# Attention in a macaron block: the score tiles on the diagonal share PSUM banks, and a group's exponentials are cut into 48 strips in place of 56

## The chip, the cores and the metric

The kernel runs on one core of one Trainium2 chip. Its time is the device time of one execution in microseconds: the median of three runs before the change is 1180.17 us (1180.03 to 1180.23). The four compute engines (TensorE or PE, VectorE or DVE, ScalarE or ACT, GpSimd or POOL) and the queue engine (SyncE or SP) each run their own instructions in order and wait for one another on semaphores. Everything here is float32, except the queries and keys of the attention, which are float16 features.

## The reference

A macaron block: half a feed-forward layer with routing to 2 of 16 experts, causal attention, half a feed-forward layer again. The change is in the attention alone, for 2 batches of 2048 tokens and 16 heads.

```python
L_q, L_k = exterior(q1, q2), exterior(k1, k2)      # 6 numbers a head and token, normalized
attn = jnp.einsum('bqhc,bkhc->bhqk', L_q, L_k @ _J6.T) * 6.0 ** (-0.5)
attn = jnp.where(causal, attn, -jnp.inf)           # a query sees the keys up to itself
attn = jax.nn.softmax(attn, axis=-1)
v = (x @ W_v + b_v).reshape(B, T, H, 16)
out = jnp.einsum('bhqk,bkhd->bqhd', attn, v).reshape(B, T, D)
x = x + out @ W_o + b_o                            # x was normalized ahead of this
```

## The kernel before, in words

Four heads make a group; there are 4 groups a batch, so `ALL` = 8 groups one after the other, numbered 0 to 7. In a group the 2048 queries are cut into `QC` = 4 chunks of 512 columns, and the keys into 16 tiles of 128. A **unit** is one chunk against one key tile for all four heads, four score tiles of 128 keys by up to 512 queries. Chunk `qc` has `4 * qc + 4` units, 40 in a group; the last four key tiles of a chunk lie on the diagonal, and of them only 512, 384, 256 and 128 columns are computed.

The score tiles go through the engines as follows.

- PE computes them (`scores`, L1880): a product over 32 rows and 128 keys, with head h on rows 32h to 32h + 31. Two slots of three PSUM banks hold them. What fills one slot is a **strip**, at most three score tiles, and a step of a group is the work for one strip.
- ACT takes the exponential of one strip with one instruction (L2021), into a ring of 8 strips in SBUF (`probs`, the tensor `wide`). It must wait until PE has used what stood there.
- POOL zeroes the triangle above the diagonal in the masked units (L2037).
- PE multiplies the values with the exponentials (`weigh`, L1905; the trace shows two records for each of the four products of a unit, one a head), and adds a chunk up in bank 6 or 7. The values carry a part whose product is the sum of the exponentials.
- DVE divides (L2069 to L2080): copy, shuffle, reciprocal, product. PE projects with `W_o` (`project`, L1919), and DVE adds to the residual (L2094).

The order on PE is written out: in step i, `scores(i)`, then the `weigh` of the units whose `pv_step` is i, then what else is due (a projection, transposes of the routing). `scores(i)` waits for exponential i - 2. Before, `strips_of` chooses the strips by a dynamic program with a cost of 152 columns a strip. It keeps the order of the units and gives a strip the columns of its widest tile. `PV_LAGS` is a table of how many steps after its last strip each unit is weighed. The projections stand at the steps of `PROJECT_7`, `PROJECT_6` and `PROJECT_6_LATE`; the ones of `PROJECT_7` in every group but the first, the others in every second group.

Of the kernel before, what the change touches and what calls it, by code (L numbers as in the profile page):

```python
# [25 lines left out]
BT = 4  # L26
# [11 lines left out]
STRIP_RING, STRIP_WIDE = 8, 3  # L38
# [1219 lines left out]
def lines(nc, core, w, tag, ctx, y_slots, q_dram, k_dram, v_dram, lent):  # L1258
# [278 lines left out]
    def vector(dve):  # L1537
# [89 lines left out]
        def split_lines(n, ring):  # L1627
# [28 lines left out]
STRIP_COST = 152  # L1656


PV_LAGS = (5, 5, 4, 4,
# [3 lines left out]

PROJECT_7, PROJECT_6, PROJECT_6_LATE = (30, 34), (39, 45, 49, 54), (49, 51, 53, 54)


def strips_of(first_columns, wide, multiple):

    count = len(first_columns)
    best = [{0: (0, None)}]  # L1670
    for end in range(1, count + 1):
        here = {}
        for n in range(1, min(wide, end) + 1):
            cost = n * (QW - min(first_columns[end - n:end])) + STRIP_COST
# [12 lines left out]

def attend(nc, core, w, tag, ctx, lines_sem, rest, v_stored, q_dram, k_dram, v_dram, xn_rows, second, routing, second_w):
# [17 lines left out]
    score = [banks[:, WIDE * n:WIDE * (n + 1), :] for n in range(SLOTS)]  # L1706
    out_bank = [banks[:, 6 + qc % 2, :] for qc in range(QC)]
# [5 lines left out]
    per_chunk = QW // P  # L1713
    units = [(qc, kt, max(0, kt - per_chunk * qc) * P) for qc in range(QC) for kt in range(per_chunk * (qc + 1))]
    U = len(units)
    last_of = [max(u for u, v in enumerate(units) if v[0] == qc) for qc in range(QC)]
    diagonal = [u for u, (qc, kt, _) in enumerate(units) if kt >= per_chunk * qc]

    strips = strips_of([c0 for _, _, c0 in units for _ in range(HG)], WIDE, RING)
    N = len(strips)  # L1720
    strip_of = [i for i, (_, n, _) in enumerate(strips) for _ in range(n)]
    place_of = [i % RING * WIDE + j for i, (_, n, _) in enumerate(strips) for j in range(n)]
    last_strip = [strip_of[HG * u + HG - 1] for u in range(U)]
    first_strip = [strip_of[HG * (last_of[qc - 1] + 1 if qc else 0)] for qc in range(QC)]

    pv_step = [last_strip[u] + lag for u, lag in enumerate(PV_LAGS)]
    assert all(a <= b for a, b in zip(pv_step, pv_step[1:]))
    pv_at = {i: [u for u in range(U) if pv_step[u] == i] for i in range(max(pv_step) + 1)}
    for i in range(N):
        assert pv_step[(strips[i][0] + strips[i][1] - 1) // HG] <= i + RING - 2  # L1730
    pieces = []
    for u in diagonal:
        runs = []
        for h in range(HG):
            at = place_of[HG * u + h]
            if runs and runs[-1][1] == at:
                runs[-1][1] = at + 1
            else:
                runs.append([at, at + 1])
        pieces.append(runs)  # L1740
    masks_of = {u: sum(len(runs) for runs in pieces[:n + 1]) for n, u in enumerate(diagonal)}
    MASKS = masks_of[diagonal[-1]]
# [6 lines left out]
    def projected_before(two, qc, half):  # L1749
# [7 lines left out]
    weights_at, logits_at, logits_turn_at, count_at, exp_at = (GATE, 41), (GATE + 1, 41), (GATE + 1, 45), (GATE + 2, 52), (GATE + 2, 6)  # L1757
    assert max(i for g, i in (logits_at, logits_turn_at)) < min(PROJECT_6_LATE) and turn_at.keys().isdisjoint({(GATE + 1, i) for i in range(29, 38)})
    rest_uses = sorted([*turn_at, weights_at, logits_at, logits_turn_at, count_at])

    late_at = {(0, 4): 0, (0, 6): 1, (0, 12): 2, (0, 15): 3}
    late_bank = lambda part: banks[:, 7 - part // 2, :]
    kept_at = {(0, 5): 0, (0, 7): 1, (0, 13): 2, (0, 16): 3}
    copied_at = (0, 2)
    assert pv_step[last_of[0]] < 12 and pv_step[last_of[0] + 1] > 6 and pv_step[last_of[1] + 1] > 15
# [56 lines left out]
    def sync(sp):  # L1822
# [27 lines left out]
        for g in range(ALL - 1):  # L1850
            for m in range(QC - 1):
                sp.wait_ge(sem.scores_ready, N * g + last_strip[last_of[m]] + 1)
                sp.sem_inc(sem.load_turn, 1)
                load_q(sp, g + 1, m)
            for m in range(QC):
                sp.wait_ge(sem.pv_done, U * g + last_of[QC - 2] + 1 + (m + 1) * BT)
                sp.sem_inc(sem.load_turn, 1)
                load_kv(sp, g + 1, m)
                if g == GATE and m < QC - 1:
                    store_normal(m)  # L1860
            load_q(sp, g + 1, QC - 1)
            if g == GATE:
                store_normal(QC - 1)
            if g == GATE + 1:
                load_shared(sp)

    def tensor(pe):
        def scores(g, i):
            first, n, c0 = strips[i]
# [12 lines left out]
            last.then_inc(sem.scores_ready, 1)  # L1882

        def weigh(g, side, two, u, uses):
# [122 lines left out]
    def scalar(act):  # L2007
        def group(g, side, two):
            for i, (first, n, c0) in enumerate(strips):
                act.wait_ge(sem.scores_ready, N * g + i + 1)  # L2010
                if i >= RING:
                    held = (strips[i - RING][0] + strips[i - RING][1] - 1) // HG
                    act.wait_ge(sem.pv_done, U * g + held + 1)
                elif later(g):
                    held = (strips[N + i - RING][0] + strips[N + i - RING][1] - 1) // HG
                    act.wait_ge(sem.pv_done, U * (g - 1) + held + 1)
# [3 lines left out]
                at = i % RING * WIDE  # L2020
# [6 lines left out]
        groups(group)  # L2027

    def gpsimd(pool):
        def group(g, side, two):  # L2030
            for u, runs in zip(diagonal, pieces):
                c0 = units[u][2]
                pool.wait_ge(sem.exp_done, N * g + last_strip[u] + 1)
                pool.sem_inc(sem.mask_turn, 1)
                for begin, end in runs:
                    part = probs[:, begin:end, c0:c0 + P]
                    pool.affine_select(out=part, in_=part, compare_op=ALU.is_ge, fill=0.0, base=0,  # L2037
                                       pattern=[[0, end - begin], [1, P]], channel_multiplier=-1).then_inc(sem.masked, 1)
# [682 lines left out]
```

## Time and profile before the change

| | us |
|---|---|
| median of three runs | 1180.17 |
| the profiled execution | 1177.99 |
| its span in the trace | 1176.3 |
| attention, first to last exponential (L2021) | 378.8 to 903.3 |
| busy: PE, ACT, DVE, POOL | 1036.9, 884.8, 774.8, 435.5 |
| exponentials of the attention (448) | 505.5 |

Of the span, 378.8 us lie ahead of the first exponential and 273 us behind the last. The first feed-forward layer and the second one are not touched. In the attention nothing is read or written in bulk: the 16 DMA engines are busy for 5 to 17% of a group.

### The profile page before, as it was taken

The numbers are of one execution on the slowest core, as the hardware profiler recorded it, in microseconds if no ns is written. First come the engines' busy times: TensorE is split into PE (matmuls) and PEld (weight loads), VectorE is DVE, ScalarE is ACT, GpSimd is POOL, SyncE is SP. The second block draws the span as 40 slices with busy tenths as digits, with TensorE's granted clock in tenths as the row PEclk, the third lists the DMA queues.
The fourth block names the chain that finished last, engine by engine and source line by source line (L and its number), as shares of the span: only waits on it lengthen the run. The fifth ranks groups of instructions, "written<-read, shape, count | busy, mean of one in ns | idle before, by whom it ended". The sixth has DMA issues, their size and how long they took to land.

```text
span 1176.3 us, 23514 instructions
## 1 busy us (share of the span) xinstructions
PE 1036.9 (88%) x7487; PEld 557.7 (47%) x7487; DVE 774.8 (66%) x1565; ACT 884.8 (75%) x1314; POOL 435.5 (37%) x531
## 2 busy tenths in 40 slices
PE   4998999898886888998889898988889998999996
PEld 3457999755553211222122122222123568898854
DVE  6897777768996314443244557476579778777866
ACT  4336777646888999999999999989998336677720
POOL 1004666377720323321111122430121435577755
PEclk9999999989998899999999999999999999999998
DMA  8902555446766101010201022020200854566655
GB/s 289 289 27 60 166 172 167 144 121 197 214 193 215 52 20 53 19 50 10 64 10 46 23 69 76 22 80 8 58 1 1 272 185 149 158 185 186 178 170 152
DMA packets 125716, 133.78 MB, mean 114 GB/s; under 512 B 13224, under 2 KB 111888, under 8 KB 125616
## 3 DMA queue, kind: packets, MB, share of 16 engines
q1 hardware_dynamic: 109056, 90.95, 24.5%
q0 software_dynamic: 14448, 39.47, 12.2%
q10 hardware_dynamic: 2112, 2.10, 0.5%
q8 instruction: 55, 0.90, 0.3%
q14 instruction: 45, 0.37, 0.1%
HBM read 80.43 MB, written 52.04 MB: 113 GB/s over the span
## 4 chain that ended last, share of the span: by engine, by line
PE 25%; ACT 23%; issue 19%; DVE 9%; POOL 2%; DVEq 1%; DMA 1%; ACTq 0%; POOLq 0%
ACT wide L2021 21%; PE banks L2388 6%; PE banks L2313 4%; PE banks L1905 3%; PE banks L2400 3%; PE banks L1880 2%; POOL f_region L1341 2%; PE banks L2322 2%; PE banks L1919 1%; PE banks L2376 1%; DVE x_res L1595 1%; DVE wide L1622 1%; DVEq L2596 1%; PE banks L1433 1%; DVE attn_lines_parts L202 1%
## 5 line engine op out<-in xcount | busy, mean ns | idle before, releaser
L2021 ACT ACTIVATE wide<-banks 128x1536 f32<-128x1536 f32 (+1 forms) x448 | 505.5, 1282 | 14.6 <-PE banks L1880 14.4
L1905 PE MATMUL banks<-wide,attn_attend_v_now 128*32 128x512 f32 (+3 forms) x2560 | 298.6, 542 | 0.1
L2037 POOL TENSOR_SCALAR_AFFINE_SELECT wide<-wide 128x512 f32<-128x512 f32 (+2 forms) x176 | 89.5, 523 | 444.3 <-ACT wide L2021 443.9
L1880 PE MATMUL banks<-attn_attend_q_now,attn_attend_k_now 32*128 32x512 f16 (+3 forms) x1280 | 158.8, 357 | 68.1 <-ACT wide L2021 64.3
L1880 PEld LDWEIGHTS banks<-attn_attend_q_now,attn_attend_k_now 32*128 32x128 f16 x1280 | 43.2, 91 | 321.2 <-ACT wide L2021 297.6
L651 POOL DMA_INDIRECT f_region<-xn_rows,f_token_of x79 | 79.1, 1001 | 126.0 <-DVE f_token_of L882 83.7
L2388 PE MATMUL banks<-f_xnt 128*128 128x128 f32 x752 | 101.7, 278 | 9.8 <-DVE f_more L2614 7.2
L2074 DVE RECIPROCAL below<-below 128x512 f32<-128x512 f32 x32 | 107.3, 3353 | 1.1
L2388 PEld LDWEIGHTS banks<-f_xnt 128*128 128x128 f32 x752 | 91.3, 191 | 15.3 <-ACT f_xnt L2466 8.8
L2069 DVE COPY sums<-banks 128x512 f32<-128x512 f32 x32 | 22.1, 691 | 109.9 <-PE banks L1905 109.1
L2496 POOL DMA_INDIRECT last_rows_in<-xn_rows,f_spare x72 | 69.7, 968 | 64.3 <-DVE f_stage L2557 23.7
L2094 DVE TENSOR_TENSOR x_res<-banks,x_res 128x512 f32<-128x512 f32 x30 | 20.7, 690 | 105.9 <-PE banks L1919 105.9
L2466 ACT ACTIVATE f_xnt<-last_w_all 128x514 f32 x94 | 59.4, 632 | 37.7 <-issue 27.4
L520 PE MATMUL banks<-f_region,wide 128*128 128x128 f32 x632 | 85.4, 279 | 0.0
L1905 PEld LDWEIGHTS banks<-wide,attn_attend_v_now 128*32 128x32 f32 x2560 | 51.6, 108 | 68.6 <-issue 61.7
L520 PEld LDWEIGHTS banks<-f_region,wide 128*128 128x128 f32 x632 | 77.8, 194 | 1.8 <-issue 0.6
L1341 POOL DMA_INDIRECT f_region<-y_slots,attn_lines_rows_of x64 | 69.8, 1090 | 23.6 <-issue 17.1
L619 ACT ACTIVATE wide<-f_w_all 128x514 f32 x79 | 50.0, 632 | 30.5 <-issue 29.5
L2599 DVE COPY last_w_down<-last_w_all 128x512 f32 x94 | 42.3, 450 | 23.2 <-issue 17.1
L2400 PE MATMUL banks<-last_w_down,f_more 128*128 128x256 f32 x188 | 56.3, 381 | 1.4 <-DVE f_more L2614 1.4
L897 DVE COPY wide<-f_w_all 128x512 f32 x79 | 38.1, 482 | 20.6 <-issue 20.2
L531 PE MATMUL banks<-wide 128*128 128x256 f32 x158 | 47.1, 381 | 0.4 <-DVE wide L910 0.4
(365 smaller groups left out, 1774.1 us busy)
## 6 DMA issues: line engine op xcount, KB each, us to landing
y_half<-f_xnt SPq DMA_DIRECT2D x94, 128.0 KB
y_slots<-wide SPq DMA_DIRECT2D x79, 128.0 KB, 1.7
attn_v<-f_more SPq DMA_DIRECT2D x32, 256.0 KB, 3.7
attn_attend_v_now<-attn_v SPq DMA_DIRECT2D x32, 256.0 KB, 3.1
x_res<-L_attn_x SPq DMA_DIRECT2D x8, 512.0 KB, 7.6
xn_rows<-f_w_all SPq DMA_DIRECT2D x8, 512.0 KB, 4.5
attn_q<-attn_lines_q_out SPq DMA_DIRECT2D x8, 512.0 KB, 3.4
attn_k<-attn_lines_k_out SPq DMA_DIRECT2D x8, 512.0 KB, 4.0
```

The source lines that it names most:

```text
L520: last = pe.matmul(bank[2 + m][:, f * P:(f + 1) * P], w_up[:, at, col_at:col_at + INTER], rows_t[:, m, c * P:(c + 1) * P], start=(c == 0), ...
L651: pool.indirect_dma_start(out=rows_in[:, n % ROUND, :], out_offset=None, in_=xn_rows, in_offset=bass.IndirectOffsetOnAxis(ap=token_of[:, n ...
L1341: pool.indirect_dma_start(out=back[:, q, j, k, :], out_offset=None, in_=y_slots, in_offset=bass.IndirectOffsetOnAxis(ap=rows_of[:, q, j, k ...
L1880: last = pe.matmul(score[i % SLOTS][:, j, c0:QW], k_now[rows, kt * P:(kt + 1) * P], q_now[rows, qc * QW + c0:(qc + 1) * QW], start=True, s ...
L1905: last = pe.matmul(out_bank[qc][rows, c0:QW], v_now[:, kt, rows], probs[:, place_of[HG * u + h], c0:QW], start=(kt == 0), stop=(u == last_ ...
L2021: act.activation(probs[:, at:at + n, c0:QW], score[i % SLOTS][:, 0:n, c0:QW], ACT.Exp, scale=SCALE).then_inc(sem.exp_done, 1)
L2037: pool.affine_select(out=part, in_=part, compare_op=ALU.is_ge, fill=0.0, base=0, pattern=[[0, end - begin], [1, P]], channel_multiplier=-1 ...
L2074: dve.reciprocal(below[:], below[:]).then_inc(sem.chain_step, 1)
L2388: last = pe.matmul(bank[2 + m][:, f * P:(f + 1) * P], w_up[:, at, col_at:col_at + INTER], rows_t[:, m, c * P:(c + 1) * P], start=(c == 0), ...
L2400: pe.matmul(bank[4 + m][:, 0:D], prod_t[:, at, :], w_down[:, at, 0:D], start=True, stop=True).then_inc(sem.y_done, 1)
L2466: act.activation(w_up[:, n % ROUND, :], w_all[:, bass.ds(expert, 1), 0:UP].rearrange("p o f -> p (o f)"), ACT.Copy).then_inc(sem.up_kept, 1)
L2496: pool.indirect_dma_start(out=rows_in(n), out_offset=None, in_=xn_rows, in_offset=bass.IndirectOffsetOnAxis(ap=s.token_of[:, place_of_turn ...
```

## The change

The strips are made by `units_and_banks`. Every chunk's masked units stand behind the first 0, 3, 5 or 9 of its other key tiles, and ahead of the rest of them. The 16 masked score tiles of a chunk take 12 banks and 4 strips: in the first two strips each bank but the third holds a tile of 512 columns, in the last two a tile of 384 columns and, in the remaining 128 columns, the tile of the last unit of the same head. The third bank of each of the four holds a tile of 256 columns. So a strip is 1536 or 1280 columns, all of them contiguous, and ACT reads it as one row (before: a pattern of up to three parts). The table `PV_LAGS` goes; a unit is weighed 2 steps after its last strip, or 4 where it is masked, and never ahead of the one before. POOL makes 10 small cuts a chunk. The projections, and the routing's transposes that are woven in, are given new steps.

```diff
-STRIP_COST = 152
-PV_LAGS = (5, 5, 4, 4,
...
-PROJECT_7, PROJECT_6, PROJECT_6_LATE = (30, 34), (39, 45, 49, 54), (49, 51, 53, 54)
-def strips_of(first_columns, wide, multiple):
...
+LAG, MASKED_LAG = 2, 4
+UNITS_AHEAD = (0, 3, 5, 9)
+HALF_HEADS = (2, 0, 3, 1)
+PROJECT_7, PROJECT_6, PROJECT_6_LATE = (24, 28), (33, 38, 42, 46), (42, 43, 45, 46)
+def units_and_banks():
+    units, banks = [], []
+    for qc in range(QC):
+        own = range(BT * qc, BT * qc + BT)
+        ahead, behind = range(UNITS_AHEAD[qc]), range(UNITS_AHEAD[qc], BT * qc)
+        for kt in (*ahead, *own, *behind):
+            units.append((qc, kt, max(0, kt - BT * qc) * P))
+        of = {kt: len(units) - 1 - n for n, kt in enumerate(reversed((*ahead, *own, *behind)))}
+        banks += [[(of[kt], h, 0)] for kt in ahead for h in range(HG)]
+        assert len(banks) % STRIP_WIDE == 0
+        one, two, three, four = (of[kt] for kt in own)
+        for n, half in enumerate(HALF_HEADS):
+            for h in (2 * n % HG, 2 * n % HG + 1):
+                banks.append([(one, h, 0)] if n < 2 else [(two, h, 0), (four, h, QW - P)])
+            banks.append([(three, half, 0)])
+        banks += [[(of[kt], h, 0)] for kt in behind for h in range(HG)]
+    return units, banks
...
-    pv_step = [last_strip[u] + lag for u, lag in enumerate(PV_LAGS)]
+    pv_step = [last_strip[u] + (MASKED_LAG if u in diagonal else LAG) for u in range(U)]
+    pv_step = [max(pv_step[:u + 1]) for u in range(U)]
...
-    turn_at = {(GATE, 45): (0, 0), (GATE, 49): (0, 1), (GATE, 52): (1, 0), (GATE, 54): (1, 1),
-               (GATE + 1, 13): (2, 0), (GATE + 1, 16): (2, 1), (GATE + 1, 24): (3, 0), (GATE + 1, 28): (3, 1)}
+    turn_at = {(GATE, 38): (0, 0), (GATE, 42): (0, 1), (GATE, 44): (1, 0), (GATE, 46): (1, 1),
+               (GATE + 1, 10): (2, 0), (GATE + 1, 12): (2, 1), (GATE + 1, 19): (3, 0), (GATE + 1, 23): (3, 1)}
...
         def scores(g, i):
...
-            for j in range(n):
-                qc, kt, _ = units[(first + j) // HG]
-                h = (first + j) % HG
-                rows = slice(h * HR, (h + 1) * HR)
-                last = pe.matmul(score[i % SLOTS][:, j, c0:QW], k_now[rows, kt * P:(kt + 1) * P],
-                                 q_now[rows, qc * QW + c0:(qc + 1) * QW], start=True, stop=True)
+            for j, parts in enumerate(score_banks[WIDE * i:WIDE * (i + 1)]):
+                for u, h, column in parts:
+                    qc, kt, c0 = units[u]
+                    rows = slice(h * HR, (h + 1) * HR)
+                    last = pe.matmul(score[i % SLOTS][:, j, column:column + columns(u)], k_now[rows, kt * P:(kt + 1) * P],
+                                     q_now[rows, qc * QW + c0:(qc + 1) * QW], start=True, stop=True)
...
-                act.activation(probs[:, at:at + n, c0:QW], score[i % SLOTS][:, 0:n, c0:QW], ACT.Exp, scale=SCALE).then_inc(sem.exp_done, 1)
+                act.activation(probs_flat[:, at:at + width_of[i]], score_flat[i % SLOTS][:, 0:width_of[i]], ACT.Exp, scale=SCALE
+                               ).then_inc(sem.exp_done, 1)
...
+                for n in range(BT):
+                    at = (strip + n) % RING * WIDE
+                    pool.wait_ge(sem.exp_done, N * g + strip + n + 1)
+                    pool.sem_inc(sem.mask_turn, 1)
+                    cut(pool, probs[:, at:at + 2, 0:P])
+                    if n >= 2:
+                        cut(pool, probs[:, at:at + 2, QW - P:QW])
+                    cut(pool, probs[:, at + 2:at + 3, 0:P])
```

On PE, the order around the end of chunk 1 in group 0, before. `attn_attend_q_now,attn_attend_k_now` are scores (their last number is the columns), `wide,attn_attend_v_now` a unit that is weighed, `ident,f_xnt` transposes left over from the layer ahead.

```order
L1880 MATMUL banks<-attn_attend_q_now,attn_attend_k_now 128x128 x3
L1880 MATMUL banks<-attn_attend_q_now,attn_attend_k_now 128x512 x3
L1905 MATMUL banks<-wide,attn_attend_v_now 32x384 x4
L1880 MATMUL banks<-attn_attend_q_now,attn_attend_k_now 128x512 x3
L1905 MATMUL banks<-wide,attn_attend_v_now 32x256 x4
L1880 MATMUL banks<-attn_attend_q_now,attn_attend_k_now 128x512 x3
L1905 MATMUL banks<-wide,attn_attend_v_now 32x128 x4
L1880 MATMUL banks<-attn_attend_q_now,attn_attend_k_now 128x512 x3
L1905 MATMUL banks<-wide,attn_attend_v_now 32x512 x4
```

The same place now, steps 12 to 16, with the score products of two strips in the first row.

```order
L1872 MATMUL banks<-attn_attend_q_now,attn_attend_k_now 128x512 x6
L1898 MATMUL banks<-wide,attn_attend_v_now 32x512 x4
L1872 MATMUL banks<-attn_attend_q_now,attn_attend_k_now 128x512 x6
L1898 MATMUL banks<-wide,attn_attend_v_now 32x384 x4
L1898 MATMUL banks<-wide,attn_attend_v_now 32x256 x4
L1898 MATMUL banks<-wide,attn_attend_v_now 32x128 x4
L1898 MATMUL banks<-wide,attn_attend_v_now 32x512 x4
L1872 MATMUL banks<-attn_attend_q_now,attn_attend_k_now 128x512 x3
L1898 MATMUL banks<-wide,attn_attend_v_now 32x512 x4
```

The three narrow masked units stood one a step, each behind the scores of a strip; now all three and the next unit of 512 columns stand in one step, with no scores between them. This is so at steps 7, 15, 27 and 47 of every group.

On ACT, one group's exponentials before, from chunk 2 on (`128x3x384` is a strip of three parts of 384 columns).

```order
L2021 ACTIVATE wide<-banks 128x1536 x12
L2021 ACTIVATE wide<-banks 128x3x384
L2021 ACTIVATE wide<-banks 128x2x384
L2021 ACTIVATE wide<-banks 128x3x256
L2021 ACTIVATE wide<-banks 128x3x128
L2021 ACTIVATE wide<-banks 128x128
L2021 ACTIVATE wide<-banks 128x1536 x17
L2021 ACTIVATE wide<-banks 128x1024
```

The same group now, from chunk 1's last strip on.

```order
L2012 ACTIVATE wide<-banks 128x1536 x7
L2012 ACTIVATE wide<-banks 128x1280 x4
L2012 ACTIVATE wide<-banks 128x1536 x16
L2012 ACTIVATE wide<-banks 128x1280 x4
L2012 ACTIVATE wide<-banks 128x1536 x4
```

A group had 37 strips of 1536 columns and 19 of 1152 down to 128, and 70,528 columns; it has 32 of 1536 and 16 of 1280, and 69,632 columns.

## Rows read from the trace of the kernel before

**Rows 1.** The page's costliest groups, attention's.
```profile
L2021 ACT ACTIVATE wide<-banks 128x1536 f32<-128x1536 f32 (+1 forms) x448 | 505.5, 1282 | 14.6 <-PE banks L1880 14.4
L1905 PE MATMUL banks<-wide,attn_attend_v_now 128*32 128x512 f32 (+3 forms) x2560 | 298.6, 542 | 0.1
L1880 PE MATMUL banks<-attn_attend_q_now,attn_attend_k_now 32*128 32x512 f16 (+3 forms) x1280 | 158.8, 357 | 68.1 <-ACT wide L2021 64.3
```

**Rows 2.** Stretches of one group: length, busy PE PEld DVE ACT POOL, clock, DMA, GB/s.
```profile
448.83:513.39 64.56, 58.44 (x508) 15.81 (x504) 28.48 (x29) 63.10 (x57) 20.58 (x27) 1.00 0.12 35
513.39:577.42 64.03, 54.41 (x492) 13.23 (x488) 24.64 (x24) 62.98 (x58) 10.77 (x22) 1.00 0.11 32
...
706.01:774.66 68.65, 62.73 (x544) 18.21 (x540) 38.90 (x49) 63.53 (x57) 21.16 (x28) 1.00 0.17 52
774.66:839.16 64.50, 54.85 (x494) 13.30 (x490) 41.27 (x68) 63.28 (x59) 11.44 (x22) 1.00 0.14 41
839.16:903.80 64.64, 58.55 (x509) 15.93 (x505) 49.71 (x82) 63.15 (x56) 12.54 (x24) 1.00 0.05 14
...
378.79:448.78 69.99, 54.74 (x482) 13.77 (x486) 19.91 (x24) 67.97 (x63) 19.66 (x24) 0.93 0.14 45
```

**Rows 3.** Exponentials alone, stretches from one start to another: busy (x), clock, DMA.
```profile
550.67:573.28 22.61, 22.61 (x17) 1.00 0.14 42
514.67:515.57 0.90, 0.90 (x2) 1.00 0.01 2
515.57:516.58 1.01, 1.01 (x2) 1.00 0.00 0
516.58:517.27 0.69, 0.69 (x2) 1.00 0.00 0
```

**Rows 4.** Timeline of PE, group 2, steps 35 to 39: start, us, engine, what.
```profile
551.62 0.39 PE L1880 MATMUL banks<-attn_attend_q_now,attn_attend_k_now 32*128 32x512 f16 x3
551.94 0.85 PE L1905 MATMUL banks<-wide,attn_attend_v_now 128*32 128x384 f32 x8
552.72 0.39 PE L1880 MATMUL banks<-attn_attend_q_now,attn_attend_k_now 32*128 32x512 f16 x3
553.04 0.86 PE L1905 MATMUL banks<-wide,attn_attend_v_now 128*32 128x256 f32 x16
553.84 0.39 PE L1880 MATMUL banks<-attn_attend_q_now,attn_attend_k_now 32*128 32x512 f16 x3
554.16 1.07 PE L1905 MATMUL banks<-wide,attn_attend_v_now 128*32 128x512 f32 x8
555.15 0.39 PE L1880 MATMUL banks<-attn_attend_q_now,attn_attend_k_now 32*128 32x512 f16 x3
```

**Rows 5.** Timeline, group 2, full strips: three exponentials from 541.60, scores of step 27.
```profile
541.60 4.24 ACT L2021 ACTIVATE wide<-banks 128x1536 f32<-128x1536 f32 x3
...
543.21 0.39 PE L1880 MATMUL banks<-attn_attend_q_now,attn_attend_k_now 32*128 32x512 f16 x3
```

**Rows 6.** Timeline, group 2 to 3: an exponential that waited for its scores.
```profile
576.93 0.39 PE L1880 MATMUL banks<-attn_attend_q_now,attn_attend_k_now 32*128 32x512 f16 x3 [0.35 <-ACT wide L2021]
...
577.37 1.45 ACT L2021 ACTIVATE wide<-banks 128x1536 f32<-128x1536 f32 x1 [0.20 <-PE banks L1880]
```

**Rows 7.** Timeline of PE, group 2: a projection, and the scores behind it.
```profile
547.50 1.13 PE L1919 MATMUL banks<-attend_w_o,heads 128*128 128x256 f32 x4
548.56 0.28 PE L1880 MATMUL banks<-attn_attend_q_now,attn_attend_k_now 32*128 32x256 f16 x3
```

**Rows 8.** Timeline: the first scores, five tiles of heads 0, 1, 2, 3, 0.
```profile
375.76 0.14 PEld L1880 LDWEIGHTS banks<-attn_attend_q_now,attn_attend_k_now 32*128 32x128 f16 x5 [2.37 <-issue]
375.79 1.01 PE L1880 MATMUL banks<-attn_attend_q_now,attn_attend_k_now 32*128 32x512 f16 x5 [2.13 <-ACT attn_lines_k_out L1496]
```

**Rows 9.** The same view around those first scores.
```profile
376.00:380.00 4.00, 0.80 (x5) 0.00 (x0) 3.34 (x5) 2.95 (x4) 0.00 (x0) 0.50 1.04 337
...
384.00:388.00 4.00, 3.98 (x28) 1.52 (x27) 0.00 (x0) 3.57 (x5) 1.40 (x3) 0.50 0.00 0
```

**Rows 10.** Groups by shape on POOL, the masks.
```profile
L2037 POOL TENSOR_SCALAR_AFFINE_SELECT wide<-wide 128x512 f32<-128x512 f32 x80 | 52.7, 660 | 431.4 <-ACT wide L2021 431.4
L2037 POOL TENSOR_SCALAR_AFFINE_SELECT wide<-wide 128x128 f32<-128x128 f32 x48 | 14.0, 293 | 12.9 <-ACT wide L2021 12.4 <-issue 0.3
```

**Rows 11.** The page's DMA issues: KB each, median us to landing.
```profile
attn_attend_v_now<-attn_v SPq DMA_DIRECT2D x32, 256.0 KB, 3.1
```

**Rows 12.** The chain that ended last, behind the attention: start, us, what.
```profile
906.27 0.70 DVE sums L2069
907.15 0.73 DVE below L2072
907.91 3.36 DVE below L2074
911.30 0.76 DVE sums L2077
912.08 0.69 DVE heads L2080
```

**Rows 13.** Timeline of the attention's end.
```profile
903.17 2.36 PE L1905 MATMUL banks<-wide,attn_attend_v_now 128*32 128x512 f32 x32
...
903.29 0.49 ACT L2021 ACTIVATE wide<-banks 128x384 f32<-128x384 f32 x1 [0.61 <-PE banks L1880]
...
906.27 0.69 DVE L2069 COPY sums<-banks 128x512 f32<-128x512 f32 x1
```

More of the change, by code:

```diff
@@ L1710, in attend @@
     q_loaded, kv_loaded = ring_semaphores(nc, f"{tag}_q_loaded", QC), ring_semaphores(nc, f"{tag}_kv_loaded", QC)
-    per_chunk = QW // P
-    units = [(qc, kt, max(0, kt - per_chunk * qc) * P) for qc in range(QC) for kt in range(per_chunk * (qc + 1))]
-    U = len(units)
+    units, score_banks = units_and_banks()
+    U, N = len(units), len(score_banks) // WIDE
+    assert len(score_banks) == N * WIDE and N % RING == 0
     last_of = [max(u for u, v in enumerate(units) if v[0] == qc) for qc in range(QC)]
-    diagonal = [u for u, (qc, kt, _) in enumerate(units) if kt >= per_chunk * qc]
@@ L1719, in attend @@
[L1719 to L1724, printed above, removed]
-    pv_step = [last_strip[u] + lag for u, lag in enumerate(PV_LAGS)]
-    assert all(a <= b for a, b in zip(pv_step, pv_step[1:]))
+    diagonal = [u for u, (qc, kt, _) in enumerate(units) if kt >= BT * qc]
@@ new lines, in attend @@
+    first_column = lambda u: units[u][2]
+    columns = lambda u: QW - first_column(u)
+    place_of = {(u, h): (b % (RING * WIDE), column) for b, parts in enumerate(score_banks) for u, h, column in parts}
+    strip_of = {(u, h): b // WIDE for b, parts in enumerate(score_banks) for u, h, _ in parts}
+    last_strip = [max(strip_of[u, h] for h in range(HG)) for u in range(U)]
+    first_strip = [min(strip_of[u, h] for u, v in enumerate(units) if v[0] == qc for h in range(HG)) for qc in range(QC)]
@@ L1728, in attend @@
+    width_of = [(WIDE - 1) * QW + max(column + columns(u) for u, _, column in score_banks[WIDE * i + WIDE - 1]) for i in range(N)]
+    held_by = [max(u for parts in score_banks[WIDE * i:WIDE * (i + 1)] for u, _, _ in parts) for i in range(N)]
+    pv_step = [last_strip[u] + (MASKED_LAG if u in diagonal else LAG) for u in range(U)]
+    pv_step = [max(pv_step[:u + 1]) for u in range(U)]
     pv_at = {i: [u for u in range(U) if pv_step[u] == i] for i in range(max(pv_step) + 1)}
     for i in range(N):
-        assert pv_step[(strips[i][0] + strips[i][1] - 1) // HG] <= i + RING - 2
@@ L1731, in attend @@
[L1731 to L1742, printed above, removed]
+        assert pv_step[held_by[i]] <= i + RING - 1
+    blocks = [(qc, strip_of[last_of[qc - 1] + 1 + UNITS_AHEAD[qc] if qc else 0, 0]) for qc in range(QC)]
@@ L1744, in attend @@
+    MASKS_OF_BLOCK = 10
+    masks_of = {u: MASKS_OF_BLOCK * units[u][0] + (3 if units[u][2] == 0 else MASKS_OF_BLOCK) for u in diagonal}
+    MASKS = MASKS_OF_BLOCK * QC
     two_of_0, four_of_1 = ((0, 0), (0, 1)), ((1, 0), (1, 1), (2, 0), (2, 1))
@@ L1904, in weigh @@
                 rows = slice(h * HR, (h + 1) * HR)
-                last = pe.matmul(out_bank[qc][rows, c0:QW], v_now[:, kt, rows], probs[:, place_of[HG * u + h], c0:QW],
+                place, column = place_of[u, h]
+                last = pe.matmul(out_bank[qc][rows, c0:QW], v_now[:, kt, rows], probs[:, place, column:column + columns(u)],
                                  start=(kt == 0), stop=(u == last_of[qc]))
@@ L2008, in group @@
         def group(g, side, two):
-            for i, (first, n, c0) in enumerate(strips):
+            for i in range(N):
                 act.wait_ge(sem.scores_ready, N * g + i + 1)
                 if i >= RING:
-                    held = (strips[i - RING][0] + strips[i - RING][1] - 1) // HG
-                    act.wait_ge(sem.pv_done, U * g + held + 1)
+                    act.wait_ge(sem.pv_done, U * g + held_by[i - RING] + 1)
                 elif later(g):
-                    held = (strips[N + i - RING][0] + strips[N + i - RING][1] - 1) // HG
-                    act.wait_ge(sem.pv_done, U * (g - 1) + held + 1)
+                    act.wait_ge(sem.pv_done, U * (g - 1) + held_by[N + i - RING] + 1)
                 if (g, i) == exp_at:
@@ L2027, in scalar, with cut @@
         groups(group)
+    def cut(pool, part):
+        pool.affine_select(out=part, in_=part, compare_op=ALU.is_ge, fill=0.0, base=0,
+                           pattern=[[0, part.shape[1]], [1, P]], channel_multiplier=-1).then_inc(sem.masked, 1)
     def gpsimd(pool):
         def group(g, side, two):
[L2031 to L2038, printed above, removed]
+            for qc, strip in blocks:
+                u = last_of[qc]
+                for n in range(BT):
[6 more added lines that the diff above has]
+                    cut(pool, probs[:, at + 2:at + 3, 0:P])
                 if g < 2 and u in (last_of[1], last_of[2]):
```

35 lines of the change are left out of this document (9 added, 26 removed), and 3 rows, old and new, of the table PV_LAGS.

## The prediction

> **What bounds the kernel now.** I read the page's list of costly groups first, then the attention stretch by stretch, then the timeline of one group. The list [rows 1] shows the attention's three large terms: 505.5 us of exponentials on ACT, 298.6 us of products with the values and 158.8 us of scores on PE. PE waits 64.3 us for ACT there, ACT only 14.4 us for PE. So ACT leads, and PE follows with little to spare. By stretch [rows 2] a group takes 64.03 us (even) or 64.56 us (odd), PE is busy for 54 to 58 us of it and ACT for 63, at the full clock (1.00). Group 5, into which the routing's products are woven, takes 68.65, group 0, with a slow start, 69.99.
>
> Busy time hides what ACT waits, since its record runs a little into the next one. The starts say more [rows 3]: 17 strips of 1536 columns take 22.61 us, 1.33 each. 1024 columns take 0.90, 1152 take 1.01, 768 take 0.69. That is a line: 0.05 us a strip and 0.833 us per 1000 columns. A group's 37 full strips are then 49.2 us, and its 19 others (4 of 1152, 2 of 1024, 5 of 768, 3 of 512, 4 of 384, 1 of 128) 12.4, together 61.6. The measured 64.03 is 2.4 us more: that is what ACT waits in a group, at the narrow strips, where an exponential is shorter than PE's step.
>
> **PE's step** is what the change has to be weighed with. In [rows 4] scores take 0.32 us to the products behind them (551.62 to 551.94), a unit of 512 columns 0.99 to the next scores (554.16 to 555.15), of 384 columns 0.78, of 256 and 128 together 0.80. Each of these ends holds about 0.10 us that is paid once, when the engine goes back to scores (the start of the scores behind a unit against the spacing of its products). So a step with one full unit is 1.31 to 1.33 us, exactly as long as ACT's 1.33. PE has no speed in reserve in such a step, only a lead. The lead: scores of step 27 start at 543.21, exponential 25 at 541.60 and 26 one strip later, at 542.93 [rows 5]. So scores start 0.27 us after the exponential before last has started its successor; an exponential that waits starts 0.44 us behind its scores [rows 6]. A strip is ready 0.27 + 0.44 = 0.71 us after the start of the one before it, 0.62 us ahead of need.
>
> **The change part by part**, for one group.
>
> *Strips.* 32 of 1.33 and 16 of 1280 columns. The trace has no strip of 1280; the bounds are its neighbours, 1.01 (1152) and 1.33 (1536), and the line gives 1.12, which I take. Sum 42.5 + 17.9 = 60.4 us, 1.2 less than 61.6. The narrow strips' waits, 2.4 us, go too. If PE kept up, a group would take 60.4.
>
> *The heavy step.* Steps 7, 15, 27 and 47 now hold the products of 384, 256, 128 and 512 columns. From the scores to the next scores: 0.32 + (0.78 - 0.10) + (0.80 - 0.10) + 0.99 = 2.69 us. The step before each is empty, so PE comes in with its full lead. The next exponential starts at 2.69 + 0.44 = 3.13 after the scores of the heavy step; ACT could start it at 2 x 1.33 - 0.27 = 2.39. It waits 0.74 us, four times: 3.0 us.
>
> *The steps behind it.* After steps 7 and 47 come two steps with a full unit each, PE 1.33, while ACT has strips of 1280, 1.12. With no lead left, 4 x 0.21 = 0.8 us. After 15 and 27 the strips are full, and this costs nothing. Then an empty step restores the lead.
>
> *Scores of one head behind one another.* Strips 3 and 4 of each masked block hold five tiles, on rows of heads 0, 0, 1, 1, 3. The trace has such a pair once: five tiles of heads 0, 1, 2, 3, 0 [rows 8], where one 512-column record is 0.6 us and the five together 1.01. The second tile of head 0 came 0.4 us later, at a clock of 0.50 [rows 9], so a tile on the same rows waits for the columns of the first. At full clock, heads in order, the chain is 384 + 384 + 256 columns at 0.42 us per 1000, 0.43 us in place of 0.21, and 0.2 later. It counts where PE has no lead, once after step 7 and once after 47: 0.4 us. Bounds: 0, and 0.3 for all columns in a row.
>
> The Trainium skill, "TensorE: Matmul & The Clock Gate", Part 3, "The mechanism", says that a weight load overlaps products in flight only on other row groups. In [rows 8] all five loads lie within 0.14 us, the fifth beside the product of its own rows, so the trace doesn't agree. By the rule each pair would also pay a load of some 0.09 us, 0.18 a strip and about 3 us over the kernel. My sum goes without it.
>
> *Projections.* One costs 1.06 us [rows 7], 0.10 of it the return to scores. At step 24 nothing else stands and the lead covers it. Step 28 has a unit too and follows the heavy step and a full one, without lead: 0.32 + 0.89 + 1.06 = 2.27 against 1.33, 0.94 us of waiting. In odd groups step 33 is alike but with a lead: 2.27 - 1.33 - 0.60 = 0.3. Step 42 stands between strips of 1280, behind the scores of one head: 0.4.
>
> *Masks.* 10 cuts a chunk in place of 5 or 6. One block is 0.29 us and four are 0.66 [rows 10]; two blocks lie between, about 0.41. A strip's cuts sum to 1.1 us, the units are weighed three strips later, so this is hidden. If it weren't, PE would stand with every unit behind it. The last keys and values of a group to come free, tiles 8 to 11, do so at step 49 and are read from the next group's step 13 on, 12 strips or 15 us later; such a load lands in 3.1 us [rows 11]. DVE's chain of a chunk, 906.27 to 912.77 [rows 12], 6.5 us, has 6 strips (8 us) at the tightest place, chunk 3 to chunk 0.
>
> *Sum.* Even group: 60.4 + 3.0 + 0.8 + 0.4 + 0.9 = 65.5, plus 0.1 where a strip of 1280 uses up the lead: 65.6, 1.6 more than now. Odd: 66.3, 1.8 more. Groups 2 and 4: 3.2; group 6 (64.50 now): 1.1; groups 1 and 3: 3.6. Group 5 has its projections at other steps and 4.1 us of extra waits now; I see as many after, 0. Group 0 has no projections, and chunk 3's heavy step counts in the next group: 60.4 + 2.2 + 0.4 + 0.2 against 61.6 + 2.4, -0.8; its first heavy step falls near 388 us, up to which the clock is 0.50 [rows 9], and 1.3 us longer products there make it +0.5. Group 7 from first to last exponential: 66.3 less the last strip (1.33) and the wait behind it (0.74), 64.2 against 64.1 now, +0.1. The end: now the last exponential starts at 903.29, and DVE copies at 906.27, 3.0 us later, held up by its own work [rows 13]; this copy is on the last chain [rows 12]. Then, PE has the heavy step and two full units left: 0.27 + 0.32 + 0.68 + 0.70 + 3 x 0.90 + 0.1 = 4.8 after exponential 46, so 3.5 after exponential 47, with DVE free. +0.5. Sum: 3.2 + 1.1 + 3.6 + 0.5 + 0.1 + 0.5 = 9.0 us. The rounding of the small waits (each cost that I took low by a few hundredths recurs 32 times) leans upwards, so I take 10. The profiled execution took 1177.99 us, 1.7 above its span and 2.2 below the median of the runs; 1188 by its own time, 1190 by the median.
>
> **The rivals.**
>
> A. *ACT alone decides.* PE's lead spans the heavy step, and every group takes 60.4: 7 x 3.8 + 4 = 31 us less, 1149. For it: ACT waits only 14.4 us now, PE waits 64.3. Against it: those 64 us lie in empty steps, and two PSUM slots let PE run no more than 0.6 us ahead.
>
> B. *The changed order costs less than written*: the pair of one head overlaps (-0.4 a group), and projection and unit pack tighter (the 0.10 is paid less often). -0.7 x 8: 1184. The other end of the same uncertainty, half of the waits real, gives no change, 1180.
>
> C. *A second wait behind the heavy step*: in group 0 more than one of its steps falls into the slow clock; in groups 5 and 7 DVE's routing work delays copies for which the woven products and projections now wait after fewer steps; and the load of the skill's rule. +2, +2, +3: 1197.
>
> **How the numbers follow.** My forecast has 0.62, A 0.05, B 0.14 (of it 0.04 for about no change), C 0.17; 0.02 for a partial gain between A and B. A measurement tells 0.2%, 2.4 us, from no change. Slower by more than that is the forecast, C and most of B, 0.90; the same 0.04; faster 0.06. The range runs from B to a little over C, 1184 to 1198; it leaves out A and the small cases, and the top of C.
>
> **What would show it.** The exponentials' own time falls to about 60.4 a group by starts, 483 us in all, while a group grows to 65.6 or 66.3. ACT's waits for scores rise from 14.4 to some 35 to 45 us, in pieces of 0.7 at exponentials 8, 16, 28 and 0, and 0.9 at 29. The timeline shows 2.7 us between the scores of steps 7 and 8. Wrong would be: a 1280 strip far from 1.12; no wait at exponential 8; waits of PE on masks or on DVE; a group under 64.

## The result, and the profile after

The changed kernel takes 1212.03 us (median of four runs, 1202.82 to 1214.77) against 1180.1 before (median of four as well): 1.0261 times as long, interval 1.0203 to 1.0319. That is slower, as forecast, but three times the forecast 10 us and outside the range of 1184 to 1198. The profiled execution took 1214.2 us.

The page's costliest groups after, beside [rows 1]:

```profile
L2012 ACT ACTIVATE wide<-banks 128x1536 f32<-128x1536 f32 (+1 forms) x384 | 499.1, 1416 | 54.7 <-PE banks L1872 51.8
L1898 PE MATMUL banks<-wide,attn_attend_v_now 128*32 128x512 f32 (+3 forms) x2560 | 309.7, 589 | 0.0
L2022 POOL TENSOR_SCALAR_AFFINE_SELECT wide<-wide 128x256 f32<-128x256 f32 (+1 forms) x320 | 114.1, 386 | 438.0 <-ACT wide L2012 435.4
L1872 PE MATMUL banks<-attn_attend_q_now,attn_attend_k_now 32*128 32x512 f16 (+3 forms) x1280 | 158.2, 376 | 75.0 <-ACT wide L2012 65.1
```

ACT's own work fell from 505.5 to 499.1 us, but its waits for scores rose from 14.4 to 51.8. PE's products with the values, the same number of the same shapes, rose from 298.6 to 309.7. The second line is the one to stop at: work that didn't change takes longer.

One row a group (groups 0 to 7, the last up to its last exponential), with the columns of [rows 2]:

```profile
380.06:452.99 72.93, 57.70 (x497) 15.24 (x501) 20.20 (x24) 67.36 (x54) 23.11 (x44) 0.84 0.14 43
452.99:520.55 67.56, 59.37 (x508) 16.91 (x509) 28.39 (x29) 62.24 (x48) 23.18 (x44) 0.95 0.11 32
520.55:590.88 70.33, 59.54 (x492) 15.26 (x493) 24.25 (x23) 62.34 (x49) 13.69 (x40) 0.88 0.11 31
590.88:659.49 68.61, 60.35 (x508) 17.02 (x508) 32.61 (x41) 62.34 (x49) 13.89 (x40) 0.93 0.11 32
659.49:730.17 70.68, 61.59 (x510) 16.59 (x511) 34.97 (x56) 62.15 (x48) 16.86 (x41) 0.88 0.15 46
730.17:799.84 69.67, 62.02 (x544) 18.73 (x545) 36.67 (x48) 62.76 (x48) 23.89 (x45) 0.98 0.15 47
799.84:870.43 70.59, 59.80 (x494) 14.75 (x495) 39.56 (x63) 62.44 (x50) 14.00 (x40) 0.88 0.14 42
870.43:938.42 67.99, 57.71 (x473) 15.82 (x473) 48.93 (x82) 60.99 (x47) 18.78 (x42) 0.92 0.05 14
```

The granted clock was 1.00 in groups 1 to 7 before; it is 0.88 to 0.98 now. Groups 1 to 6 take 67.6 to 70.7 us where I had 65.6 and 66.3. From first to last exponential the attention takes 558.4 us in place of 524.5, 33.9 of the 36.2 us between the two profiled executions; 1.3 lie ahead of it and 0.8 behind.

PE in group 3, from the unit of step 1 to the scores of step 8 (start, us, what, and the idle time before it):

```profile
592.07 1.07 PE L1898 MATMUL banks<-wide,attn_attend_v_now 128*32 128x512 f32 x8
593.07 0.81 PE L1872 MATMUL banks<-attn_attend_q_now,attn_attend_k_now 32*128 32x384 f16 x10
594.90 0.39 PE L1872 MATMUL banks<-attn_attend_q_now,attn_attend_k_now 32*128 32x512 f16 x3 [1.02 <-ACT wide L2012]
595.94 0.39 PE L1872 MATMUL banks<-attn_attend_q_now,attn_attend_k_now 32*128 32x512 f16 x3 [0.65 <-POOL wide L2022]
596.26 1.06 PE L1898 MATMUL banks<-wide,attn_attend_v_now 128*32 128x512 f32 x8
597.28 0.49 PE L1872 MATMUL banks<-attn_attend_q_now,attn_attend_k_now 32*128 32x512 f16 x3
598.62 0.61 PE L1872 MATMUL banks<-attn_attend_q_now,attn_attend_k_now 32*128 32x512 f16 x3 [0.85 <-ACT wide L2012]
599.16 4.50 PE L1898 MATMUL banks<-wide,attn_attend_v_now 128*32 128x384 f32 x32
603.59 0.61 PE L1872 MATMUL banks<-attn_attend_q_now,attn_attend_k_now 32*128 32x512 f16 x3
```

and the same stretch by busy time and clock (steps 2 to 4 with the scores of step 5; step 5's unit to the scores of step 7; the heavy products; what follows), with the exponential that waited:

```profile
593.07:596.26 3.19, 1.50 (x21) 0.45 (x17) 2.87 (x4) 3.10 (x4) 1.88 (x6) 1.00 0.51 147
596.26:599.16 2.90, 2.05 (x17) 0.36 (x14) 2.67 (x2) 2.90 (x3) 0.79 (x3) 0.70 0.66 200
599.16:603.59 4.43, 4.43 (x35) 1.39 (x33) 1.40 (x3) 2.09 (x2) 0.00 (x0) 0.50 0.02 4
603.59:607.50 3.91, 3.69 (x36) 0.79 (x32) 3.84 (x3) 3.04 (x3) 1.14 (x4) 0.91 0.00 0
```
```profile
604.25 1.24 ACT L2012 ACTIVATE wide<-banks 128x1280 f32<-128x1280 f32 x1 [2.99 <-PE banks L1872]
```

Steps 2 to 4 hold scores and nothing else: PE is busy for 1.50 of 3.19 us. In the next stretch the clock falls to half (1.2 GHz), at about 597.4 by its mean of 0.70 over 596.26 to 599.16, and the heavy step is taken at half clock, 4.43 us of products in place of the 2.4 of my sum. ACT idles for 2.99 us ahead of exponential 8; by starts, the way I had counted, it is 3.16 us late, not 0.74. The trace's record of the clock has twenty such falls between the first and the last exponential, eighteen of them behind the idle steps 2 to 4, 10 to 12 and 22 to 24. The kernel before has none after its slow start.

### The profile page after: what moved, and what is told of

It reads as the page before. It is cut to its first block, busy times and chain, and to the rows that moved or that the text cites. A ratio compares the mean times of both kernels' runs of the same rounds, so it can differ in the third digit from the quotient of the medians.

```text
span 1212.2 us, 23530 instructions
## 1 busy us (share of the span) xinstructions
PE 1058.3 (87%) x7487; PEld 569.8 (47%) x7487; DVE 771.3 (64%) x1565; ACT 879.0 (73%) x1250; POOL 458.2 (38%) x675
## 3 DMA queue, kind: packets, MB, share of 16 engines
q1 hardware_dynamic: 109056, 90.95, 23.7%
## 4 chain that ended last, share of the span: by engine, by line
PE 38%; ACT 14%; issue 12%; DVE 12%; POOL 2%; DVEq 1%; DMA 1%; ACTq 0%; POOLq 0%
PE banks L1898 14%; ACT wide L2012 13%; PE banks L2386 6%; PE banks L1872 5%; PE banks L2311 4%; PE banks L2398 3%; PE banks L1912 2%; POOL f_region L1341 2%; PE banks L2320 2%; DVE x_res L1595 1%; PE banks L2374 1%; DVE wide L1622 1%; DVEq L2594 1%; DVE attn_lines_parts L202 1%; DVE attn_lines_line L1633 1%
## 5 line engine op out<-in xcount | busy, mean ns | idle before, releaser
L2012 ACT ACTIVATE wide<-banks 128x1536 f32<-128x1536 f32 (+1 forms) x384 | 499.1, 1416 | 54.7 <-PE banks L1872 51.8
L1898 PE MATMUL banks<-wide,attn_attend_v_now 128*32 128x512 f32 (+3 forms) x2560 | 309.7, 589 | 0.0
L2022 POOL TENSOR_SCALAR_AFFINE_SELECT wide<-wide 128x256 f32<-128x256 f32 (+1 forms) x320 | 114.1, 386 | 438.0 <-ACT wide L2012 435.4
L1872 PEld LDWEIGHTS banks<-attn_attend_q_now,attn_attend_k_now 32*128 32x128 f16 x1280 | 39.0, 92 | 316.6 <-ACT wide L2012 218.6
L1898 PEld LDWEIGHTS banks<-wide,attn_attend_v_now 128*32 128x32 f32 x2560 | 64.7, 118 | 86.0 <-issue 79.5
L2494 POOL DMA_INDIRECT last_rows_in<-xn_rows,f_spare x72 | 69.9, 971 | 65.5 <-DVE f_stage L2555 23.7
```

The lines of the kernel that those rows point to most:

```text
L1872: last = pe.matmul(score[i % SLOTS][:, j, column:column + columns(u)], k_now[rows, kt * P:(kt + 1) * P], q_now[rows, qc * QW + c0:(qc + 1) ...
L2012: act.activation(probs_flat[:, at:at + width_of[i]], score_flat[i % SLOTS][:, 0:width_of[i]], ACT.Exp, scale=SCALE).then_inc(sem.exp_done, 1)
L2494: pool.indirect_dma_start(out=rows_in(n), out_offset=None, in_=xn_rows, in_offset=bass.IndirectOffsetOnAxis(ap=s.token_of[:, place_of_turn ...
```

## The experiments

All of these ran on another chip, on which the layers outside the attention take some 70 to 87 us longer (653.8 us of the changed kernel's span on the first chip, 723.6 to 741.1 in the eight profiles here): the kernel before takes 1261.54 us in the first set (23 runs) and 1253.78 in the second (19). So ratios are read within a set, and beside them the **attention time**, first to last exponential in the profile; it was 524.5 us before and 558.4 after, both on the first chip; the kernel before has no profile on the second. "Waits" are differences of exponentials' starts less the strip's own time (0.05 us and 0.833 us per 1000 columns). My first theory was that idle steps make the clock fall (1); the rivals were that the heavy step costs this by itself (2), or that the new strips do (3).

### Idle steps filled

```diff
+        def fill(g, side, two, i):
+            if g in (0, 5) or i not in (2, 3, 4, 10, 11, 12):
+                return
...
+            for _ in range(3):
+                pe.matmul(banks[:, 6, :], k_now[:, 0:P], k_now[:, 0:QW], start=True, stop=True)
```

> The changed kernel with three extra products of 128 rows, 128 keys and 512 columns (float16, into the idle bank 6, result unused) behind the scores of steps 2, 3, 4, 10, 11 and 12 of groups 1, 2, 3, 4, 6 and 7. They add PE work and remove only idleness. Theory 1 (the clock falls because steps 2 to 4 and 10 to 12 leave PE idle, and the heavy steps 7 and 15 then run at half clock): the granted clock in those groups returns to 1.00 at steps 7 and 15, the waits there shrink from 2 to 3 us to 0.5 to 0.8, a group takes 65 to 66.5 us in place of 68 to 70.5, and the whole 1190 to 1200 us (groups 0 and 5 unchanged). Rival, theory 2 (the heavy step itself, whatever stands before it, costs 2 to 3 us, through the products' queue or the masks): time unchanged at 1203 to 1215 or longer by what the extra products take.

Measured: 1.0117 times before (1.0060 to 1.0174), attention 541.1 us. In all six groups where they were filled, the falls at steps 2 to 7 and 10 to 15 are gone, and the waits at exponentials 8 and 16 are 0.59 us each. Ten falls in place of twenty are left, all where nothing was filled: group 0, group 5, and around steps 23, 24 and 45. So more work on PE makes the kernel faster (554.3 us of attention unfilled on this chip, see below); theory 2 predicted no gain or a loss.

### The rest of the idle steps filled

```diff
+            six, seven = i in (2, 3, 4, 10, 11, 12), i in (22, 23)
+            late = i in (43, 44) and side == 0 and g != GATE
```

> The changed kernel with idle steps filled as in the first filled run, and also steps 22 and 23 of every group, 43 and 44 of groups 0, 2 and 6, and 2 to 4 of group 5; the extra products' result is unused. Theory 1 (idle steps make the clock fall): of the ten falls that the first filled run kept, those at steps 23, 24 and 44 and in group 5 go, leaving group 0's. Attention falls from 541.1 to about 528 to 533 us, which is what my step arithmetic gave at full clock (525 to 536), and every group but 0 and 5 has clock 1.00 and takes 65 to 66 us. Theory 2: the waits at 24, 25 and 47 stay.

Measured: 1.0093 (1.0059 to 1.0126), attention 534.4 us. Groups 1 to 3, and PE's heavy step in group 3:

```profile
476.20:541.50 65.30, 61.68 (x532) 17.91 (x528) 28.43 (x29) 62.12 (x49) 23.48 (x44) 1.00 0.11 33
541.50:606.40 64.90, 59.16 (x522) 15.54 (x519) 24.29 (x23) 61.99 (x48) 13.69 (x40) 1.00 0.12 34
606.40:671.80 65.40, 61.78 (x532) 17.99 (x536) 32.53 (x41) 62.17 (x49) 14.13 (x40) 1.00 0.11 33
```
```profile
609.72 0.39 PE L1872 MATMUL banks<-attn_attend_q_now,attn_attend_k_now 32*128 32x384 f16 x5
...
614.52 2.36 PE L1898 MATMUL banks<-wide,attn_attend_v_now 128*32 128x384 f32 x32
616.81 0.39 PE L1872 MATMUL banks<-attn_attend_q_now,attn_attend_k_now 32*128 32x512 f16 x3
```

The heavy products take 2.29 us to the next scores, against 4.43 in the changed kernel, and a group 65.0 or 65.3. These groups are what my prediction described: the same order with the clock at 1.00. The whole run is not quite that. I expected one fall to be left, in group 0; there are three, in groups 0, 5 and 7:

```profile
430.40:433.80 3.40, 3.40 (x31) 1.07 (x27) 0.54 (x1) 1.44 (x2) 0.87 (x1) 0.50 0.07 19
754.70:758.10 3.40, 3.40 (x22) 0.47 (x23) 0.35 (x1) 2.48 (x2) 0.00 (x0) 0.50 0.13 39
935.60:942.40 6.80, 6.42 (x39) 2.86 (x43) 3.12 (x13) 3.15 (x3) 2.13 (x3) 0.50 0.01 2
```

Beside the same places without a fall they cost 1.5 us at exponential 16 of group 0 (2.12 against 0.59 in the other groups), 1.0 at exponential 14 of group 5 (no wait there in the first filled run) and 1.2 at exponential 47 of group 7 (1.45 against 0.29). Attention is 9.9 us longer than the 524.5 of before (the medians of this set differ by 10.9). Less these 3.7 us, the order at full clock throughout would cost about 6.2, an estimate; my sum had 8.5 for the attention.

### The changed kernel again, in the same set

> The changed kernel, unchanged, beside the others on one chip. Attention 553 to 562 us, 20 or so falls of the clock; 25 to 35 us slower than before. If the falls were an accident of the first chip, the time would be within 10 to 15 us of before.

Measured: 1.0226 (1.0134 to 1.0317), 28 us by this ratio and 23.7 at the medians, attention 554.3 us, 17 falls. In one set, then, 19.9 us of attention lie between the order with its idle steps and the order with them filled (12.8 us between the medians of whole runs). The runs also show it by themselves: their mean granted clock goes with their time, 1202.82 us at 0.956, 1209.85 at 0.951, 1214.2 and 1214.77 at 0.945 on the first chip.

### One unit a step earlier

```diff
+    pv_step = [5, 6, 7, 7, 7, 8, 9, 13, 14, 15, 15, 15, 16, 17, 19, 20, 21, 25, 26, 27, 27,
+               27, 28, 29, 31, 32, 33, 35, 36, 37, 39, 40, 41, 45, 46, 47, 47, 47, 48, 49]
```

The changed kernel has 5, 7, 7, 7, 7 at the start of this list, and so at each of the chunks: one masked unit of each goes a step earlier.

> The changed kernel with one difference: the masked unit of 384 columns is weighed one step earlier (steps 6, 14, 26, 46), so the heavy step holds 0.68 us less, and the idle steps 2 to 4 and 10 to 12 stay as they are. Theory 1: the clock still falls about as often (mean granted clock of the groups 0.88 to 0.97, as now), and the time falls by the smaller heavy step only, some 15 to 20 us of the waits at 7, 15, 27 and 47 (2.4 us a group at full clock), to 1190 to 1199 us. Theory 2 (the heaviness alone makes the clock fall or the wait long): the clock returns to 1.00 and the time to under 1185 us.

Measured: 1.0067 (1.0035 to 1.0099), attention 530.8 us, 12 falls. Less heavy, 23.5 us shorter than the 554.3 of the changed kernel on this chip, and the clock still falls. It gained more than I expected, and it does not single out a theory: the step moved fills one gap besides.

### All masked units a step earlier

```diff
-LAG, MASKED_LAG = 2, 4
+LAG, MASKED_LAG = 2, 3
```

> The changed kernel with MASKED_LAG 3 in place of 4: masked units one step earlier. The step that held 2.5 units of products is split in 1.5 and 1, and one of the three idle steps (4, 12) now has a unit. Theory 1: fewer falls of the clock than in the changed kernel (two idle steps in a row in place of three), mean clock of the groups 0.97 to 1.00, heavy waits gone, group 62 to 64 us, whole kernel 1168 to 1182 us. Theory 2 (heaviness alone) gives the same side but cannot give a clock under 1.00; a clock that still falls with no heavy step is for theory 1.

Measured: 0.9969 (0.9940 to 0.9998), attention 514.8 us, 2 falls, groups mostly 62.4 to 63.7. One number in one line takes the kernel from 2% slower to no slower. With 0.3% it is at the edge of what can be told.

### The products spread

```diff
-    pv_step = [last_strip[u] + (MASKED_LAG if u in diagonal else LAG) for u in range(U)]
-    pv_step = [max(pv_step[:u + 1]) for u in range(U)]
+    pv_step = [5, 6, 7, 7, 8, 10, 11, 12, 14, 15, 16, 16, 17, 18, 20, 21, 23, 25, 26, 27,
+               27, 29, 30, 31, 32, 33, 35, 36, 37, 38, 39, 41, 42, 45, 46, 47, 48, 49, 50, 51]
```

> The changed kernel with its strips, masks and projections, but a table of steps for the products with the values: at most one full unit a step, none of the steps 2 to 4 and 10 to 12 in a row empty. Theory 1 and the arithmetic of steps: no heavy step and no idle stretch, clock 1.00, a group takes 60.5 to 62 us, and the whole kernel 1155 to 1163 us, faster than both. Theory 3 (the new strips themselves cost more than the line of 0.05 us and 0.833 us per 1000 columns, or tiles that share a bank slow PE or ACT): a group stays over 64 us and the kernel over 1180.

Measured: 0.9886 (0.9858 to 0.9914), 14 us faster than before, attention 509.2 us. The clock stays at 1.00 from group 1 to step 45 of group 7. So the strips are good, and theory 3 falls: with them unchanged, another table of steps takes 45 us off the attention. It is a little less than I expected, because the odd groups take 62.92 us and not under 62.

### Idleness by itself

```diff
+                if u in (5, 6, 7):
+                    last = pe.matmul(out_bank[qc][rows, QW - 32:QW], v_now[:, kt, rows], probs[:, place, QW - 32:QW], start=False, stop=False)
+                    continue
```

> The spread kernel with work left out: the products with the values of units 5, 6 and 7 (steps 10, 11 and 12 of each group) cover the last 32 columns only, so the output is not the reference's. No step is heavy. Theory 1: steps 10 to 12 are idle but for their scores, the clock falls there in most groups, and the full units of steps 14 to 17 at half clock cost ACT 1 to 3 us a group: attention as long as in the spread run or longer (509 to 525 us), although 24 products fewer are computed. Theory 2 (only a heavy step costs): the clock stays at 1.00, attention 509 us or less.

Measured: 0.9975 (0.9944 to 1.0006), attention 514.8 us, 5.6 us longer than the spread kernel of the first set with less to compute. The clock falls at this place in every one of the eight groups. Group 2, steps 1 to 8, steps 9 to 12 (step 9 has no unit in this table), the fall, and after:

```profile
537.50:547.50 10.00, 9.33 (x92) 2.17 (x92) 5.50 (x5) 10.00 (x10) 3.34 (x10) 1.00 0.36 105
547.50:552.10 4.60, 2.27 (x44) 0.90 (x40) 4.23 (x6) 4.60 (x6) 2.30 (x7) 1.00 0.01 5
552.10:558.90 6.80, 6.04 (x44) 1.44 (x44) 2.06 (x2) 6.69 (x5) 1.03 (x4) 0.50 0.08 22
558.90:564.00 5.10, 4.84 (x44) 0.86 (x36) 4.25 (x4) 4.36 (x5) 0.00 (x0) 1.00 0.00 0
```

PE was busy for 2.27 of 4.60 us, with no heavy step anywhere near, and 6.8 us at half clock followed. The fall needs only the idleness. What it costs depends on what comes then: here mostly single units, 0.4 to 1.6 us of waits at exponentials 15 to 17 of groups 1 to 4, 6 and 7, where the spread kernel has none; in the changed kernel the heaviest step of the chunk, up to 3.2 us each.

### The version that beats both

The spread table, and the odd groups' projections at steps without a full unit:

```diff
-PROJECT_7, PROJECT_6, PROJECT_6_LATE = (24, 28), (33, 38, 42, 46), (42, 43, 45, 46)
+PROJECT_7, PROJECT_6, PROJECT_6_LATE = (24, 28), (34, 40, 44, 47), (40, 43, 44, 47)
-               (GATE + 1, 10): (2, 0), (GATE + 1, 12): (2, 1), (GATE + 1, 19): (3, 0), (GATE + 1, 23): (3, 1)}
+               (GATE + 1, 10): (2, 0), (GATE + 1, 13): (2, 1), (GATE + 1, 19): (3, 0), (GATE + 1, 23): (3, 1)}
```

> The spread table of the earlier run, with the projections of the odd groups moved from steps 33, 38, 42, 46 to 34, 40, 44, 47 (group 5: 40, 43, 44, 47), steps with no product of values or a small one, and one transpose of group 5 from step 12 to 13. Arithmetic of steps: an odd group takes 62.92 us in the spread run against 60.92 for an even one, because a projection beside a full unit overruns ACT by 0.3 to 0.9; that goes. Attention 509.2 us there, some 6 to 9 less here, 500 to 503; about 21 to 24 us less than the kernel before on the same chip (524.5 in its profile). Rival: the odd groups' 2 us are waits for DVE, which moving projections does not shorten: time as in the spread run, 14 us less than before.

Measured: 0.9824 (0.9761 to 0.9886), 1229.83 us beside 1253.78, 24 us at the medians; attention 500.4 us, 24.1 less than in the profile of before on the first chip. Groups 1 to 3, and the exponentials:

```profile
472.60:533.80 61.20, 56.96 (x500) 15.46 (x504) 28.01 (x29) 61.20 (x49) 23.68 (x44) 1.00 0.12 35
533.80:594.90 61.10, 53.68 (x496) 12.82 (x493) 24.73 (x24) 61.10 (x50) 13.35 (x40) 1.00 0.12 36
594.90:656.00 61.10, 56.94 (x500) 15.44 (x504) 30.81 (x37) 61.10 (x49) 13.88 (x40) 1.00 0.13 36
```
```profile
L2014 ACT ACTIVATE wide<-banks 128x1536 f32<-128x1536 f32 (+1 forms) x384 | 491.3, 1539 | 4.6 <-PE banks L1874 3.9
```

ACT is busy in each of these stretches from end to end, and waits 3.9 us in all. The 1.8 us of groups 1 and 3 (62.92 to 61.16 by starts) were waits behind projections, not for DVE. Half of the 8.7 us gained over the spread run lie in group 7, where the fall at step 45 is gone too.

## Why the prediction was wrong, point by point

**The side and the mechanism on PE were right, and the level of the clock was missing.** The forecast was +10 us, the result +32. With most idle steps filled the changed order costs 9.9 us of attention, of which 3.7 belong to the three falls left; about 6.2 are the order at full clock, where my sum had 8.5, and 0.5 behind the attention. That 9.9 lies close to my 9.0 is luck in part. The rest is the clock: 554.3 - 534.4 = 19.9 us within one set (558.4 - 534.4 = 24.0 across the chips), and with the 3.7 about 24 to 28 us, an estimate.

**The step that failed** is "Then an empty step restores the lead", and with it "the step before each is empty, so PE comes in with its full lead". I counted the empty steps 2 to 4 and 10 to 12 as time given back. They are three in a row, which the kernel before does not have, and in the changed kernel PE is busy for only 1.50 of the 3.19 us that end at 596.26, and the clock falls about 1.2 us later, ahead of the heavy step. The rows for it were in my hands: [rows 9] show 0.50 after idle time, [rows 2] a clock of 1.00 that I took as given for the changed order too. At full clock the lead does come back, and the wait is 0.59 us; what the sum lacked is a term for the clock behind those steps. My rival C had the slow clock in group 0 only, +2.

**The terms at full clock**, from the kernel with most idle steps filled:

| term | predicted us | measured us |
|---|---|---|
| strip of 1280 columns, start to start | 1.12 | 1.118 |
| wait behind the heavy step (8, 16, 28, 0) | 0.74 each | 0.59, 0.59, 0.67, 0.70 to 0.78 |
| the two steps behind it, narrow strips | 0.21 each | 0.20, 0.21 |
| tiles of one head in a strip | 0.2 each | 0 |
| projection at step 28 | 0.94 | 1.05 |
| projections at 33 and 42, groups 1, 3 and 7 | 0.3 and 0.4 | 0.34 and 0, in group 7 1.24 at step 42, for DVE |
| even and odd group | 65.6, 66.3 | 64.98, 65.31 |
| group 0 and group 5, more than before | 0.5, 0 | 2.0, 2.0; of these 1.5 and 1.0 at half clock |

The groups that I worked out step by step were a little dear; group 0, less its fall, came out as I had it, and group 5, less its own, 1.0 us above. Behind the attention I had +0.5 us and 0.8 was measured. Masks and K/V loads cost ACT nothing that the trace shows: POOL's work rose from 89.5 (its 176 masks) to 114.1 us. The trace of the changed kernel does put 5.9 us of PE's idle time ahead of scores to POOL, nine times in groups 1 to 7, as at 595.94 above; but in the program scores wait for an exponential and not for a mask, and in group 2 the same gap, 0.65 us long too, is put to ACT. DVE is another matter. Four projections in groups 5 and 7 waited 3.3 us for its additions, and one of these waits, 1.17 us at step 42 of group 7, made exponential 43 there 1.24 us late. I had named waits of PE on DVE as a sign of being wrong; this one is real and small.

**The rivals.** A, ACT alone, was wrong for this kernel by 63 us, but its price of a group, 60.4 us by the line of [rows 3], is what the last experiment nearly reaches (61.05 to 61.16 in groups 1 to 3). B, 0.7 us less a group, missed the total, but at full clock the groups came out near it, 0.6 and 1.0 under my forecast: tiles of one head did cost nothing, and a projection beside a unit did not pack tighter. C named the slow clock, in group 0 only, at a tenth of its price; its waits for DVE in groups 5 and 7 came in part; its load of a pair, 3 us, does not show: behind the heavy step the waits are 0.20 and 0.21 us, what full steps against narrow strips give without it. My chance of 0.90 for slower was fair; the range was not, for it held no term for the clock at all.

## What to carry to other kernels

When a change moves an in-order engine's work, look at the gaps that it opens as well as at the steps that it fills. A gap on TensorE is not rest: here the clock fell to half behind three steps of scores alone, and the heaviest step, which came next, took 4.4 us in place of 2.3. Before costing a new order, mark each run of thin steps that the old one does not have and price what stands behind it at either clock; keep the work even, one unit a step; if it can't be even, idle steps are worth filling with work that nobody needs. And split such a change: with the same strips the attention took 554.3 us with the uneven table of steps and 500.4 with the even one and its moved projections.

## What the runs showed of the hardware that I had not expected

- The clock fell although PE never stood still for long: the gaps ahead of the fall in group 3 are 1.02 and 0.65 us, with scores between them, and of the changed kernel's twenty falls only two (group 0, step 15, and group 5, step 12) stand behind a longer one, 1.87 and 1.83 us. In the experiment on idleness by itself, 2.27 us of work in 4.60 went ahead of it.
- Five score tiles of heads 0, 0, 1, 1 and 3 (384, 128, 384, 128 and 256 columns) take 0.39 us of PE, no longer than three tiles of 512 on three heads, also 0.39. In the last experiment's records (group 2, at 545.16) the three tiles on free rows start within 0.013 us of one another and the second ones of heads 0 and 1 0.17 us later, so a tile that has to wait for its rows did not hold up a later one on other rows. What is left in a row is 384 + 128 columns on one head, as many as one tile of 512. I had put tiles of three heads behind one another, 0.2 us.
- The attention of the changed kernel took nearly the same time on two chips, 558.4 and 554.3 us, while the rest of the kernel took 70 us longer on the second (spans of 1212.2 and 1277.9 us). No run shows why.
